# Gathering all 128 rows of a window: the index limit taken off the indirect DMAs of a graph network kernel

## What is computed

```python
h = relu(gcn_conv(x, W1, b1, src, dst, N)); out = gcn_conv(h, W2, b2, src, dst, N)   # 128 -> 256 -> 128
# gcn_conv: segment_sum(h[src] * dinv[src] * dinv[dst], dst) + h * dinv**2 + b
x = layernorm(x + out)
att = sigmoid(xs @ W_att[:d] + xd @ W_att[d:] + b_att)       # xs = x[src], xd = x[dst]
aggregated = segment_sum((xs @ W_msg + b_msg) * att, dst)
# a GRU cell on (aggregated, x), batch norm over the nodes, and
x = layernorm(x + that)
```

## Time and profile before

| | |
|---|---|
| time, median of 3 runs | 1756.09 us (1754.35 to 1758.73) |
| the profiled execution | 1759.59 us, span 1757.5 us |
| busy in the span | PE 84%, DVE 80%, ACT 68%, POOL 60% |
| indirect gathers | 882, 294 in each of conv, norm and gru |
| software DMA queue (q0) | 39.54 MB, 9.4% of the 16 DMA engines' span |

### The profile page before, as it was taken

How to read it: one execution, slowest core, us unless ns; L and a number is a source line. 1 busy time by engine, 2 the same in 40 slices (tenths; PEclk the granted TensorE clock), 3 DMA queues, 4 the chain that set the end, 5 groups by cost and what they waited for, 6 DMA issues and landing times.

```text
span 1757.5 us, 35422 instructions
## 1 busy us (share of the span) xinstructions
PE 1473.8 (84%) x7678; PEld 1042.8 (59%) x7678; DVE 1398.1 (80%) x4668; ACT 1196.8 (68%) x3010; POOL 1053.4 (60%) x1014
## 2 busy tenths in 40 slices
PE   6300699999999958899999959999999999976765
PEld 3200477777777747778787845555555555545554
DVE  7817699999999858888888826888888888877786
ACT  6786355555555527777776746777777777757898
POOL 5000677777777547777777735666666666614442
PEclk9755799999999979999999979999999999988898
DMA  8798799998888738898776747777754444439998
GB/s 262 264 342 308 241 328 331 329 317 271 270 269 270 262 118 274 298 313 300 250 235 224 242 152 222 233 226 232 228 167 130 127 128 127 132 99 384 374 324 277
DMA packets 246942, 433.97 MB, mean 247 GB/s; under 512 B 41831, under 2 KB 44108, under 8 KB 246848
## 3 DMA queue, kind: packets, MB, share of 16 engines
q1 hardware_dynamic: 218160, 393.40, 65.8%
q0 software_dynamic: 28688, 39.54, 9.4%
HBM read 274.13 MB, written 178.01 MB: 257 GB/s over the span
## 4 chain that ended last, share of the span: by engine, by line
PE 61%; POOL 11%; DMA 11%; issue 6%; DVE 6%; ACT 4%; SPq 1%; DVEq 0%; ACTq 0%; POOLq 0%
POOL gath L695 10%; PE bank L1379 10%; PE bank L1371 10%; PE bank L1363 5%; PE bank L1431 5%; PE bank L1433 5%; PE bank L1445 5%; PE bank L1435 5%; PE bank L1438 5%; PE bank L1437 5%; DMA page<-YT 3%; PE bank L1396 3%; DMA gath<-G,ROWI 3%; ACT page L901 2%; DMA page<-in_x 2%
## 5 line engine op out<-in xcount | busy, mean ns | idle before, releaser
L695 POOL DMA_INDIRECT gath<-MT,ROWI x294 | 325.1, 1106 | 199.7 <-PE bank L1445 115.6
L695 POOL DMA_INDIRECT gath<-XP,ROWI x294 | 332.1, 1130 | 171.7 <-issue 88.7
L695 POOL DMA_INDIRECT gath<-G,ROWI x294 | 294.4, 1001 | 116.9 <-issue 83.8
L791 ACT ACTIVATE page<-bank,b_sb 128x512 f32<-128x512 f32 x196 | 124.0, 684 | 152.7 <-PE bank L1371 152.7
L1379 PEld LDWEIGHTS bank<-w_sb,page 128*128 128x128 f32 x1568 | 190.3, 192 | 46.4 <-issue 46.4
L1396 PE MATMUL bank<-gath,onehot 128*128 128x128 f32 x1176 | 161.0, 288 | 47.3 <-DMA gath<-G,ROWI 44.7
L1379 PE MATMUL bank<-w_sb,page 128*128 128x128 f32 x1568 | 190.7, 275 | 0.0
L1371 PE MATMUL bank<-page,w_sb 128*128 128x512 f32 x392 | 185.8, 597 | 0.0
L1363 PE MATMUL bank<-onehot,gath 128*128 128x170 f32 (+1 forms) x588 | 104.1, 314 | 94.9 <-DMA gath<-XP,ROWI 94.9
L1396 PEld LDWEIGHTS bank<-gath,onehot 128*128 128x128 f32 x1176 | 144.3, 198 | 51.2 <-issue 39.0
L1465 PE MATMUL bank<-ident,page 128*128 128x128 f32 x784 | 119.0, 304 | 62.2 <-DMA page<-YT 57.2
(11 more groups left out here) (224 smaller groups left out, 3292.7 us busy)
## 6 DMA issues: line engine op xcount, KB each, us to landing
page<-YT SPq DMA_DIRECT2D x196, 256.0 KB, 3.4
MT<-page SPq DMA_DIRECT2D x98, 260.0 KB, 3.3
XP<-page SPq DMA_DIRECT2D x98, 256.0 KB, 2.5
page<-in_xT SPq DMA_DIRECT2D x98, 256.0 KB
page<-DQ SPq DMA_DIRECT2D x98, 256.0 KB
G<-page SPq DMA_DIRECT2D x98, 256.0 KB
OWN<-page SPq DMA_DIRECT2D x98, 256.0 KB
page<-OWN SPq DMA_DIRECT2D x98, 256.0 KB
```

The costliest lines, as they stand in the source:

```text
L695: nc.gpsimd.indirect_dma_start(gath[k][:, w, 0:width], None, rows, bass.IndirectOffsetOnAxis(ap=ROWI[:, at:at + 1], axis=0), bounds_check= ...
L791: last = nc.scalar.activation(rows[k], bank[2 + 2 * k + h][:], ACT.Relu, bias=b1_sb[:, h:h + 1])
```

## The change

The gathers lose their limit on the index (`bounds_check`, with `oob_is_err=False`), so no lane is skipped. `SKIP` is no longer added, and all lanes hold the row of their own edge. The gather buffers are no longer cleared, as every lane is now written. The one-hot weights stay as they were, so what the extra lanes bring is multiplied by 0.

```diff
                 with pool.If(flag < 1):
-                    last_row = pool.to_reg(NP - 1)
                     stored()
...
                             nc.gpsimd.indirect_dma_start(gath[k][:, w, 0:width], None, rows,
-                                                         bass.IndirectOffsetOnAxis(ap=ROWI[:, at:at + 1], axis=0),
-                                                         bounds_check=last_row, oob_is_err=False).then_inc(landed[k], 16)
+                                                         bass.IndirectOffsetOnAxis(ap=ROWI[:, at:at + 1], axis=0)).then_inc(landed[k], 16)
...
             table_row(win_t[q], win_src[q], win_u[q])
-            link(nc.vector.tensor_copy(win_sf[q], win_t[q]))
-            link(nc.vector.scalar_tensor_tensor(win_sf[q], win_ok[q], -float(SKIP), win_sf[q], ALU.mult, ALU.add))
-            nc.vector.tensor_scalar(win_sf[q], win_sf[q], float(SKIP), None, ALU.add).then_inc(windows_f, 1)
+            nc.vector.tensor_copy(win_sf[q], win_t[q]).then_inc(windows_f, 1)
...
-            for rows in (*gath, zeros, e_msg, e_sum, e_tgt):
+            for rows in (zeros, e_msg, e_sum, e_tgt):
                 nc.vector.memset(rows[:], 0.0)
```

## The result

The changed kernel takes 1745.87 us (median of 5), the kernel before 1758.73 us in the same comparison (median of 5). The ratio of the two is 0.992, with a 95% interval from 0.9904 to 0.9937: 14 us faster (11 to 17). One execution of each kernel (1910.51 us before, 3997.1 us after) fell in the slow state and is not in the ratio. Timed once more beside new runs of the kernel before, it was 1743.06 against 1757.63 us, ratio 0.9924 (0.9909 to 0.9938). The forecast was 1760.1 us, in a range from 1749 to 1768.

A forecast was written before the change was run, and what follows sets the result against it. PE was taken to bound conv and gru, POOL norm, with DMA nearly full in conv's first part. Conv +3.4, landings +0.6 and all else 0 gave +4.0 on 1756.1: 1760.1 us, range 1749 to 1768.

The forecast's parts named there:

- What bounds each pass: PE sets the pace of conv at 4.37 us a group, POOL that of norm; in gru PE is always busy.
- The instruction on POOL: In norm, dropping the comparison saves between 0 and 34 ns on each of 294 gathers; taken as 0.
- More real lanes cost POOL nothing: Gathers on POOL take the same time however many of their 128 lanes are real: 0 us.
- The added bytes in conv: In conv's first part, DMA demand of 103.4% lengthens the period to 4.52 us; PE loses 3.4 us.
- The absorbed backlog: In conv's first part, DVE running behind hides 1.7 us of the 5.1 us DMA delay from PE.
- the loop of two slots: In conv, loads hang on DVE reading, SP issuing and the transfer landing, leaving bubbles that hold the DMA share at 0.98.
- the rival built on it: DMA engines can't be filled beyond 0.98; conv loses 6.5 us, norm 1.5, with landings +8.6: 1764.7 us, chance 0.20.
- The rival that the added bytes are hidden: In conv, DMA keeps pace with PE's 4.37 us; only landings remain, +0.6 us: 1756.7 us, chance 0.20.
- Bytes over the whole kernel: Added rows cost 3.4 us in conv and 0.6 us in landings, 4.0 us in all.
- The 0.6 us for landings: At the first and last gather of each pass, six places, a later landing costs 0.1 us each.
- DVE before the passes: Removing two DVE instructions and four memsets before the passes is worth 0, hidden under 37.16 us of idle time.
- The cheaper gathers: Rival: in norm the comparison costs the full 34 ns, POOL is 10 us faster: 1750 us, chance 0.17.

The follow-up runs named there:

- the extra store: The changed kernel, with SP in conv storing each whole own-rows tile a second time, 256 KB a group, into an unread table: 1752.7 us, ratio 0.9968.

## Why the prediction was wrong

- **What bounds each pass** was right: PE in conv and gru, POOL's back-to-back gathers in norm. The two runs with the limit in norm only and outside norm only show it for POOL: the gain is where POOL sets the pace and nowhere else.
- **The instruction on POOL: the step that failed.** "The saving lies between 0 and 34 ns. ... I take 0". It is 53 ns, and 294 x 0.053 = 15.6 us account for the measured 14 us (11 to 17). That is also the sign that the prediction named: gathers shorter than 965 ns. Three readings of the earlier trace rows misled me. The kernel has nine gathers without a limit and not six; the three of L680 into win_dst, left out, took 1.73 to 2.05 us and would have shown that this place is no undisturbed one. The 993 ns that I took as "the nearest in row size" were not the price of a gather without a limit: in the changed kernel's trace the same line, which the change doesn't touch, has one of 958 ns and one of 1.73 us. DVE was running its comparisons of two SBUF inputs beside both. These are POOL and DVE of the changed kernel (start us, us, line):

```profile
27.32 0.96 POOL L680 DMA_INDIRECT win_src<-in_src,start_i  x1 [0.31 <-issue]
28.59 1.73 POOL L680 DMA_INDIRECT win_src<-in_src,start_i  x1 [0.30 <-issue]
```

```profile
27.31 0.87 DVE L934 TENSOR_TENSOR oh_lo<-col_h,gath 128x1280 bf16<-128x1280 f16 x1 [1.13 <-PE bank L1312]
28.10 1.37 DVE L934 TENSOR_TENSOR oh_hi<-col_h,gath 128x2352 bf16<-128x2352 f16 x1
```

  What stretches the one and not the other, these rows don't show. The Trainium skill, page "GPSIMD Engine Reference" (section Specifications), says that the SBUF interfaces are shared with VectorE, with contention beside DVE instructions with two SBUF inputs. The passes agree in part: in gru, from 1060 to 1300 us, the 46 gathers that ran for 0.3 us or more beside DVE's L1213, which reads two SBUF tiles, have a median of 1.27 us, and 36 of them took 1.25 us or more; the 47 that ran for less than 0.3 us beside it and beside L1204 took at most 0.95 us. But ten of the 46 took 0.95 us or less, and no run took DVE's work away. Two gathers that follow each other, and L1213:

```profile
1200.30 0.95 POOL L694 DMA_INDIRECT gath<-MT,ROWI  x1 [0.30 <-issue]
1201.55 1.27 POOL L694 DMA_INDIRECT gath<-MT,ROWI  x1 [0.30 <-issue]
```

```profile
1201.25 0.75 DVE L1213 SCALAR_TENSOR_TENSOR page<-page,bhh_sb 128x512 f32<-128x512 f32 x1 [0.23 <-ACT page L859]
```

  And I took the 958 ns as a lower bound, "the upper end may be due to the 98 lanes", as if fewer lanes were cheaper. Without a limit, the shortest gathers on 128 lanes take 938 to 940 ns, and of those on 98 lanes none took less than 958. A bound that comes from a neighbour of another shape is no bound.
- **More real lanes cost POOL nothing** was right: the gathers with all lanes real and the limit back have the same 997 ns.
- **The added bytes in conv: 3.4 us, measured none.** This step failed too. "Over 100% can't be" took the busy share for a capacity. The share went to 1.01, and q1's packets became shorter as q0's grew. With the extra store, at 387 GB/s, it was 1.04, and there DVE waited 30 times for a load, in a stretch in which it waited for none in the changed kernel. The absorbed backlog, the loop of two slots and the rival built on it fall with it. The rival that the added bytes are hidden was right for conv. It was also the one to which the Trainium skill's page "DMA: Bandwidth & Descriptors" (section Bandwidth) led with its 435 GB/s. That section puts the figure down to SBUF's ports, and has beside it, which the prediction left out, about 358 GB/s for a core when both cores of its HBM domain stream, as what binds between HBM and SBUF. With one core at work 387 GB/s were moved here, above the second figure; no stretch reached the first, and there were waits for loads at 387.
- **Bytes over the whole kernel: 4.0 us predicted, 3.3 (1.4 to 5.1) measured** with the limit back. The size came out by luck: 3.4 of the 4.0 were put in conv, which shows no loss. The 0.6 us for landings rest on one eighth of a microsecond each, but 43 rows of 512 B at 340 GB/s are 0.065 us; no run isolates that term.
- **DVE before the passes: 0,** as measured.
- **The cheaper gathers** were the rival on the other side, with its threshold of 32 ns. The mechanism and its place were right. Its price was capped at 34 ns where 53 were measured, and the prediction gave it a chance of 0.17.

## What to carry to other kernels

Where an engine issues back to back, price its instruction to the nanosecond: what an option on it costs is multiplied by its count, here 53 ns by 294. In the passes where another engine sets the pace, the same option had no price. When the trace has the cheaper form only in other shapes or beside a busy neighbour, look at all of them and leave the bound open on both sides. In this kernel a DMA busy share of 0.98 was not yet a ceiling; such a share is a reason to look for waits on transfers, and as long as none shows, there may be room.

## What was not expected of the hardware

- An index limit that skips costs 53 ns on a gather of 128 rows (944 to 997 ns), whether or not a lane is beyond it. Set to report an error it costs 69 ns (1013 ns), with no lane beyond it; the other case wasn't run.
- Skipping lanes saves bytes and no packets: 28688 packets with and without skipping, at 39.54 and 58.89 MB.
- Two chips differ by 5% on this kernel (1757 and 1850 us). On the slower one the gathers of conv and norm come 1.52 us apart whatever their own length, with waits named remote at POOL, and gru's gathers, 1.71 us apart, run over 502 us (499 to 502 on the first). With 196 gathers in norm its pass is hardly slowed there (335.3 us from 654.2 to 989.5, and 331.2 on the first), while conv is. All of these fit a pace of POOL of no less than 1.52 us a gather on that chip. What holds them back no run here shows. Where POOL's pace was that, the length of a gather had no worth: 944 and 1013 ns gave 1852 and 1851 us.
